# Routing kept as a table in memory that is written group by group, expert weights split behind the attention, tiles added into x2 in memory

## The reference, cut to what matters

```python
NB, LQ, LC, D = 32, 112, 375, 256       # batches, queries, context rows, width
x = x + tanh(g_xattn) * attention(ctx, layernorm(x))      # 16 heads of 64; keys: ctx and x, 487 rows
xf = layernorm(x).reshape(T, D)                           # T = 32 * 112 = 3584 tokens
gate_scores = softmax(xf @ gate_w)                        # 8 experts
topk_scores, topk_idx = top_k(gate_scores, 2)
topk_scores = topk_scores / sum(topk_scores)
h = gelu(einsum('td,edf->etf', xf, w1) + b1[:, None, :])  # F = 1024
y = einsum('etf,efd->etd', h, w2) + b2[:, None, :]
out = einsum('kt,ktd->td', topk_scores.T, y[topk_idx.T, arange(T)])
return x + tanh(g_ffn) * out
```

## Time and profile before

| | us |
|---|---|
| median of 3 runs (lowest, highest) | 1881.23 (1879.61, 1881.39) |
| the profiled execution | 1880.83 |
| its span, first to last instruction | 1879.1 |
| PE busy | 1657.4 (88%) |
| DVE busy | 1348.8 (72%) |
| ACT busy | 1186.2 (63%) |
| POOL busy | 1185.2 (63%) |

### The profile page before, as it was taken

The page is one execution under the profiler, slowest core; times in us unless marked ns, Lnnn a source line. Parts: engine busy times, 40 slices in busy tenths (PEclk is TensorE's granted clock), DMA queues, the critical chain, the costliest instruction groups (busy, mean ns, idle before and its releaser), DMA issues. The chain is left out here.

```text
span 1879.1 us, 42970 instructions
## 1 busy us (share of the span) xinstructions
PE 1657.4 (88%) x15031; PEld 1161.6 (62%) x15032; DVE 1348.8 (72%) x3173; ACT 1186.2 (63%) x2666; POOL 1185.2 (63%) x1297
## 2 busy tenths in 40 slices
PE   2899999999999999999999999997303999999980
PEld 0456666666666666666666666665202999989970
DVE  5777877778777787777877778775495666666646
ACT  2587887778877787777877778776244333333320
POOL 4477778777787777877778777767163433434420
PEclk9999999999999999999999999998556999999995
DMA  4267767667777776666766667667454111111119
GB/s 132 50 132 143 152 138 139 138 142 152 138 138 138 142 153 138 136 140 142 154 138 137 139 142 142 129 128 151 124 178 154 51 45 50 47 47 50 45 36 292
DMA packets 599543, 233.20 MB, mean 124 GB/s; under 512 B 534064, under 2 KB 584016, under 8 KB 598992
## 3 DMA queue, kind: packets, MB, share of 16 engines
q1 hardware_dynamic: 592656, 212.67, 52.7%
q0 software_dynamic: 6720, 18.36, 3.2%
HBM read 78.66 MB, written 20.19 MB: 53 GB/s over the span
## 5 line engine op out<-in xcount | busy, mean ns | idle before, releaser
L279 POOL TENSOR_TENSOR p_parts<-p_f,p_parts 112x487 f16<-112x487 f32 x512 | 559.6, 1116 | 185.6 <-ACT p_parts L373 185.6
L364 ACT ACTIVATE p_f<-scores_ps,shift 112x487 f32<-112x487 f32 x512 | 337.7, 664 | 7.9 <-DVE passed L494 4.2
L494 DVE TENSOR_SCALAR_CACHE_REDUCE passed<-scores_ps 112x487 f16<-112x487 f32 x512 | 308.0, 658 | 30.2 <-PE scores_ps L645 30.2
L401 ACT ACTIVATE k_hi<-proj_ps 128x488 fp32r<-128x488 f32 x256 | 148.0, 578 | 256.1 <-PE proj_ps L627 256.0
L1010 ACT ACTIVATE space<-h_ps,b_sb,undo 128x256 f32<-128x256 f32 x280 | 142.6, 559 | 233.4 <-PE h_ps L1239 231.0
L528 DVE SCALAR_TENSOR_TENSOR v_sb<-proj_ps,v_sb 128x512 f16<-128x512 f32 (+1 forms) x256 | 176.9, 691 | 140.6 <-ACT v_sb L415 139.4
L373 ACT ACTIVATE p_parts<-p_f 112x487 f16<-112x487 f32 x512 | 275.8, 607 | 0.0
L522 DVE TENSOR_TENSOR k_lo<-proj_ps,k_hi 128x488 fp32r<-128x488 f32 x256 | 169.0, 660 | 91.4 <-ACT k_hi L401 91.2
L676 PE MATMUL pv_ps<-v_sb,pt_sb 128*128 128x128 f16 x2048 | 218.2, 221 | 7.6 <-DMA pt_sb<-p_parts 4.8
L627 PE MATMUL proj_ps<-kv_hi,wkv_hi 128*128 128x488 f16 x512 | 191.4, 374 | 28.7 <-POOL kv_lo L306 13.5
L627 PE MATMUL proj_ps<-wkv_hi,kv_hi 128*128 128x512 f16 (+1 forms) x512 | 194.3, 379 | 0.3
(11 more groups left out here) (222 smaller groups left out, 4017.1 us busy)
## 6 DMA issues: line engine op xcount, KB each, us to landing
w_part<-in_L_ffn_w_dram SPq DMA_DIRECT2D x64, 256.0 KB, 3.5
stage<-in_L_ffn_w_dram SPq DMA_DIRECT2D x32, 512.0 KB, 4.5
ctx_sb<-in_ctx_dram SPq DMA_DIRECT2D x32, 375.0 KB
space<-y_rows SPq DMA_DIRECT2D x32, 224.0 KB, 4.7
pt_sb<-p_parts SPq DMA_TRANSPOSE x256, 4.0
x_sb<-in_x_dram SPq DMA_DIRECT2D x32, 112.0 KB
res_sb<-in_x_dram SPq DMA_DIRECT2D x32, 112.0 KB, 5.3
x_dram<-x_sb SPq DMA_DIRECT2D x32, 112.0 KB, 2.9
```

What stands on the lines that cost most here:

```text
L279: pool.tensor_tensor(p_parts[0:LQ, p % PS, h, 1, 0:LK], p_f[0:LQ, p % 2, h, 0:LK], p_parts[0:LQ, p % PS, h, 0, 0:LK], ALU.subtract).then_i ...
L364: act.activation(p_f[0:LQ, p % 2, h, 0:LK], scores_ps[n][0:LQ, 0:LK], ACT.Exp, bias=shift[0:LQ, p // 2 % 2, n:n + 1], scale=-1.0, accum_ou ...
L401: act.activation(k_hi[:, j], ps[:, 0:LKP], ACT.Copy).then_inc(kq_high, 1)
L494: dve.tensor_scalar(passed[0:LQ, n], scores_ps[n][0:LQ, 0:LK], P_SHIFT, None, ALU.add, ALU.min, accum_out=shift[0:LQ, p // 2 % 2, n:n + 1] ...
```

## The change: what it does

The two parts become one program without a barrier. (1) Attention: the steps behind PV are given by a table of stages for each batch (`USUAL`, `LATE` for batch 29, `EARLY` for 30 and 31, whose last products go to their own PSUM banks), and the drain is 20 steps. (2) Routing is done inside the attention. The batches form seven groups of 8, 8, 8, 4, 2, 1 and 1. For each group DVE makes the 0/1 vectors (`choose`), PE counts with one product more than there are batches (L1210, L1212), DVE turns counts into places in a table (`rank_entries`), and POOL writes (token, weight), 8 bytes each, into a table in memory with one indirect DMA of 112 rows per batch and choice, 64 in all, a batch per step. Each expert owns 28 rows of 128 entries; entries that nobody writes name a spare row and weight 0. Behind the attention one indirect read fetches the 70 rows in use and PE transposes them. (3) The maximum of the weights' parts is taken up to step 28 * 8, the scales are computed there, and the 32 units are loaded and split at fixed steps: 0, 1, 2 at steps 250, 252, 254, units 3 to 22 one in each step from 256 on, 23 to 25 before the tiles, the last six in the iterations of the first tiles. Always ACT makes the high half and DVE the low one. PE waits only for the experts that a tile can use. (4) Tiles: all 35 are written out. ACT weighs y by the table's weight (two more instructions to a tile), and POOL adds the rows into x2 in memory by indirect DMAs with an addition; each tile's adds wait until the last tile's have landed. (5) The last stage is four copies from memory to memory, 3.67 MB.

```diff
+USUAL = dict(zip(STAGES, (13, 21, 22, 23, 24, 25, 26, 26, 27, 28, 29, 31, 32, 33)))
+EARLY = dict(zip(STAGES, (13, 14, 15, 16, 17, 18, 19, 20, 21, 22, 23, 23, 24, 25)))
+LATE = dict(USUAL, hot=27, share=28, prefix=28, rank=29, entry=30)
+GROUPS = ((0, 8), (8, 16), (16, 24), (24, 28), (28, 30), (30, 31), (31, 32))
+SPLITS = {PAIRS - 6: 0, PAIRS - 4: 1, PAIRS - 2: 2}
+SPLITS.update({PAIRS + n: 3 + n for n in range(20)})
+BEFORE_TILES = (23, 24, 25)
+TILE_SPLITS = {-2: 26, -1: 27, 0: 28, 1: 29, 2: 30, 3: 31}
+LOADS = {t + 1: u + 4 for t, u in SPLITS.items()}
+            def load_unit(u):
...
+                if 4 <= u < 28 or u == 31:
+                    sp.wait_ge(unit_low, u - 3 if u < 28 else 29)
...
+                sp.dma_start(staged, unit_source(u)).then_inc(unit_loaded[unit_slot(u)], 16)
...
+            sp.dma_start(tanh_g[:, 1:2], g_f.partition_broadcast(128)).then_inc(small_loaded, 16)
...
+                if t == PAIRS - NP - 1:
+                    for u in range(4):
+                        load_unit(u)
+                if t in LOADS:
+                    load_unit(LOADS[t])
...
+            per = TOKENS // 4
+            for n in range(4):
+                sp.dma_start(out.rearrange("b p d -> (b p) d")[n * per:(n + 1) * per].rearrange("(q r) d -> q (r d)", q=128),
+                             sums[n * per:(n + 1) * per].rearrange("(q r) d -> q (r d)", q=128)).then_inc(out_stored, 16)
...
+                for ob in entries_at(t):
...
+                    pool.wait_ge(rank_done, n + 1)
+                    for k in range(TOPK):
+                        pool.indirect_dma_start(table.rearrange("r (n w) -> (r n) w", w=2), bass.IndirectOffsetOnAxis(ap=place_i[0:LQ, ob, k:k + 1], axis=0),
+                                                entry[0:LQ, ob, k], None).then_inc(entered, 16)
+            pool.wait_ge(row_known, 1)
+            pool.wait_ge(entered, NB * TOPK * 16)
+            pool.wait_ge(out_done, NB)
+            pool.indirect_dma_start(slots_sb[0:HALVES, :], None, table, bass.IndirectOffsetOnAxis(ap=table_row[0:HALVES, :], axis=0)).then_inc(slots_read, 16)
...
+            def add(t):
+                pool.wait_ge(y_weighed, t + 1)
+                if t >= 1:
+                    pool.wait_ge(summed[(t - 1) % 2], ((t - 1) // 2 + 1) * 32)
+                for a in range(2):
+                    n = 2 * t + a
+                    pool.indirect_dma_start(sums, bass.IndirectOffsetOnAxis(ap=sums_row[:, n:n + 1], axis=0), yw_sb[:, t % 2, a], None, compute_op=ALU.add).then_inc(summed[t % 2], 16)
...
+                if t in SPLITS:
+                    unit_high_of(SPLITS[t])
...
+                for n in groups_at("prefix", t):
...
+                    nc.tensor.matmul(ps[0:LQ, 264:264 + wide], before_me[0:LQ, 0:LQ], rows[:, 0:wide], start=True, stop=False)
+                    for d in range(1, last - first + 1):
+                        final = nc.tensor.matmul(ps[0:LQ, 264 + 8 * d:264 + wide], ones[0:LQ, 0:LQ], rows[:, 0:wide - 8 * d], start=False, stop=(d == last - first))
-            pe.wait_ge(w_split, UNIT_COUNT // 4 * 3)
-            pe.wait_ge(w_split_pool, UNIT_COUNT // 4)
+                    if n < E:
+                        pe.wait_ge(unit_low, 4 * (n + 1))
```

More of the change, by code:

```diff
@@ L31 @@
 LAG = 4
+REGION = 16384
+EXPERT_WORDS = 8192
+PARTS = 4 * E
+UNIT = 1024
 def span(t):
     return t // NP, t % NP
-STEPS = range(-3 * NP, NB * NP + 3 * NP)
+STEPS = range(-3 * NP, NB * NP + 20)
 PAIRS = NB * NP
@@ new lines, in program @@
+        base = sb("base", [128, E])
+        place = sb("place", [128, 8, E])
+        picked = sb("picked", [128, 8, TOPK, E])
+        rank = sb("rank", [128, 8, TOPK])
+        place_i = sb("place_i", [128, NB, TOPK], I32)
+        entry = sb("entry", [128, NB, TOPK, 2])
+        peaks = sb("peaks", [128, PARTS, 2])
+        b1_rows = sb("b1_rows", [E * KF, 128])
+        b1_sb = sb("b1_sb", [128, E, KF])
+        table_fill = xn_sb
+        spare_fill = x2_sb
+        count_i = sb("count_i", [128, 2, E], I32)
@@ L350, in _ @@
+            for t in range(TILES + 1):
+                if t + 2 < TILES:
+                    pool.wait_ge(xt_done, t + 1)
+                    gather(t + 2)
+                if t >= 1:
+                    add(t - 1)
         @block.scalar
         def _(act):
-            act.wait_ge(small_loaded, 16 * 6)
+            act.wait_ge(small_loaded, 16 * 7)
             act.activation(tanh_g[:, :], tanh_g[:, :], ACT.Tanh).then_inc(tanh_done, 1)
@@ new lines, in _ @@
+            s_then(dve.scalar_tensor_tensor(out=reached[HS, 1], in0=tile_end[HS, :], scalar=tile_of[HS, 0:1], in1=less[HS, :], op0=ALU.is_le, op1=ALU.mult))
+            s_then(dve.tensor_reduce(found[HS, :], reached[HS, :, 0:E - 1], AX.X, ALU.add))
+            dve.tensor_scalar(table_row[HS, :], found[HS, 1:2], row_no[HS, :], None, ALU.add).then_inc(row_known, 1)
+            for u in BEFORE_TILES:
+                unit_low_of(u)
+            dve.wait_ge(slots_turned, 1)
+            dve.tensor_copy(tile_expert[:, :], tail_bank[0:1, 256:256 + HALVES:2])
@@ L694, in _ @@
-                if ob is not None:
+                for ob in batches_at("xnt", t):
+                    ended = [n for n, (first, last) in enumerate(GROUPS) if last == ob and ob < NB - 2]
+                    if ended:
+                        pe.wait_ge(placed, ended[0] + 1)
+                    if t == CHAIN + 9:
+                        pe.wait_ge(f_moved, 5)
                     pe.wait_ge(xn_done, ob + 1)
                     for k in range(KD):
-                        last = nc.tensor.transpose(tail_ps[:, k * LQ:(k + 1) * LQ], xn_sb[0:LQ, ob % 2, k * 128:(k + 1) * 128], ident[0:LQ, 0:LQ])
+                        last = nc.tensor.transpose(tail_ps(ob)[:, k * LQ:(k + 1) * LQ], xn_sb[0:LQ, ob % 2, k * 128:(k + 1) * 128], ident[0:LQ, 0:LQ])
```

1117 lines of the change are left out of this document (524 added, 593 removed).

## The result

The kernel before ran in 1880.42 us (median of 4, 1878.1 to 1881.39), the changed one in 1850.41 us (1849.45 to 1851.1): ratio 0.9841, interval 0.983 to 0.9853. The forecast was 1831 in a range of 1793 to 1868, and faster. It is faster, inside the range, and by 30 us where 49 were forecast. The span of the profiled execution went from 1879.1 to 1849.4, 29.7 less. Where these come from is read at four places, as in the prediction.

The account below looks back on a forecast made before the run. PE's products were taken to bound attention and tiles, with time to gain in the drain, routing and last stage. First h -19.8, ramp +1, end -30.6 gave -49.4 from 1879.1; plus 1.7 outside the span, 1831 us, range 1793 to 1868.

Parts of the forecast that it names:

- Entries, +24: Attention, POOL: entry DMAs at 1.28 exceed the round by 11.6 a group, less 3.4 reserve; 8 for each of three groups.
- Rival A: Entries cost POOL little: 24 becomes 4 in the attention, 11 becomes 4 in the last steps; 1804 us, chance 0.24.
- D: Rival: routing stays on POOL's path, entry DMAs costing 2.19 as beside a DVE split; +50, 1881 us, chance 0.05.
- Prefix products, +7: Attention, PE: 32 small fp32 products at up to 0.28 each, 9.0 in all; taken as +7 us, bounds 4 and 10.
- Table operations, +2: Attention, DVE: some 15 short operations per group, mostly beside PE, may delay emptying a bank; +2 us, bounds 0 and 6.
- Start, +1: Start: SP spreads one more scalar over 128 partitions ahead of DVE's first maximum; +1 us, between 0 and 3.5.
- Last steps, +11: Attention's last steps: 7 for group four's entries on POOL, 4 for unit loads; +11 us, bounds 0 and 20.
- Last PV: End of attention: the last PV moves from 1319 to 1364 through start, products, table operations, entries and last steps.
- Last PV to first h, 52.5: Routing: units' pace sets 1408, the table's path is hidden behind it; first h at 1416.5, 19.8 us earlier.
- End, 28: Behind the last y: DVE, ACT, adds, landing and a copy of 16; 28 against 58.6, -30.6 us, bounds -35 and -20.
- rival C: Tiles: serial adds set the pace, period 2.6 plus landing, counting from a landing of 8.3; at 12, 1957 us; chance 0.06.
- Ramp +1: First tile iterations: six units left to split, where DVE has some 4 us free in 10.9; +1 us, bounds 0 and 6.

Follow-up runs that it names:

- the eight traces: Traces of kernels with the changed kernel's start left as it was; the lag at batch 2 against the kernel before was 1.4 to 3.4 us.
- The new places: Unit splits moved out of batch 31's route, and copies on SP moved, against the changed kernel: 1840.06 us, ratio 0.9783 to the kernel before.

## Why the prediction was right, and where it was off

- **Entries, +24 of bounds 0 to 36.** Measured 31.6, 7.6 more, near the upper bound. The price of 1.28 was right (by rows it would have been 1.14, not the "1.2 to 1.3" beside it), and so was the excess over a round, 11.6. The step that failed is the 3.4 taken off each group as reserve behind POOL: 0.9 for ACT and 2.5 for the second bank. The groups cost 11.9, 9.9 and 9.9, so 0 to 1.7 was given in place of 3.4; which of the two terms failed wasn't isolated. Spread out, the same issues cost 2.9. Rival A (cheap entries) needed them to fit as they stood; they fit only one per round. Of D, the 2.19 beside a DVE split did not come in the middle of the attention (median 0.95); in the last steps and the route six of 16 took 1.74 to 3.56.
- **Prefix products, +7.** 0.196 each by 32 is 6.3. **Table operations, +2**: three steps of 1.1 here, 4.5 for four if the fourth is alike; which of the group's work makes them wasn't isolated. **Start, +1**: 3.0 in the profiled execution, 2.5 over the eight traces. Not priced at all: four steps of 0.5 ahead of batches 7, 11, 15 and 19. They stand behind the four extra weight parts that PART_STEPS adds at steps 33, 65, 97 and 129; that is their place only, no run took them away.
- **Last steps, +11.** 12.3, of which group 3's entries 8.9 (predicted 7) and the rest 3.4 (predicted 4).
- **Last PV** at 1377.6, not 1364: 13.6 late, of which the entries 7.6, the start 2, the extra parts 2, and 1.3 the last steps; groups 0 to 2's products and table work came to 8.6 of the 9 taken for four groups, and some 1 stays without a name.
- **Last PV to first h, 52.5.** Measured 62.6. This is the second step that failed: "writing them and reading the table back are hidden behind units 21 to 25; if units were free, that path would set 1400". The path is batch 31's norm, transposes, choice and ranks with a split in every step, and each of ten splits (1.28), and each wait for its load, delays the path's next link. I priced units and path as two lines of which the later wins; on one engine in program order they are one line. The new places show it: 10.2 earlier. And x2 stands 17.7 behind the last PV, not 11: the transpose of o, taken as 4, had landed 8.5 after its issue (1381.8 to 1390.3), at a DMA share of 0.97 from 1381 to 1391 and with unit loads on the same queue ahead and behind; that the loads made it late is likely, not shown. The units' own pace was priced well: from x2 to the last of the 26, 30.4 where 33 were taken. From there to the first h it was 14.5, not 8.5, because the table was not in. So 6.7 for x2, -2.6 for the pace and 6.0 for the path make the 10.1. The path by itself was too short as well: with 1400 in place of 1408 the first h would stand 44.5 behind the last PV, and with the splits moved it still stood 52.9 behind. "The first h set by the table's path or by DVE's order" is one of the signs of being wrong that the prediction names.
- **End, 28.** 22.0 from DVE's step behind the true last y. The copy with its completion took 13.4 where I had 19. Here the forecast was right by luck: I set 28 against 58.6, which began a tile's y too early; against the true 53.2 the forecast would have been -25. The -30.6 agrees with -31.2 because the two errors cancel. The Trainium skill ("DMA: Bandwidth & Descriptors", "Where 436 GB/s comes from") gives about 358 GB/s for a core's memory, and I took reads and writes to share it, which made 20.5 of the copy. They moved 3.67 MB each way in 13.4, 548 GB/s together, so the trace does not bear this out. The Trainium skill says in the same page, in the note under "Measured", that the figure is a core's part when both cores of a pair stream, and here one core runs.
- **Adds.** Landing 4.0 (taken: 4), POOL 1.66 each and not 1.0; the period of about 8 lies below 10.9, so rival C never came near. (With a landing of 2.3 the end would have been 1.7 earlier, not the 1.6 of the prediction.)
- **Ramp +1**: -2.4. PE waits for no unit, and the granted clock in the first 24 us was 0.88, against 0.80 before. What raised it wasn't tested.

So the stages were right in their order and the sum was 19.7 too low: +13.6 and +10.1 at the first h, -3.4 in the ramp and -0.6 at the end, of the 49.4 forecast. The time lies in the range because the range was wide (75 us), and the agreement at the end is two errors that cancel.

## What to carry to other kernels

Work put on an engine with a quarter of its time idle costs nothing only if it comes in portions that fit the idle time of one round; a burst pays nearly the whole excess of every round, and a reserve that the engine behind is thought to give should be counted as nothing until a run shows it. Filler work between the links of a latency-bound path is on the path when both run on one engine in program order: put it where that engine waits for another. Before a stage's length is taken from the chain of waits, look in the timeline whether its last product is the last one of the kernel.

## What the runs showed of the hardware

In the middle of the attention an indirect DMA of 112 rows of 8 bytes occupied POOL for 0.95 us (0.94 to 1.21), and the next started 1.25 to 1.51 behind it; with 56 rows it was 0.93 (0.91 to 1.18), and with 128 rows of 1 KB 1.00. Of the 16 in the last steps and the route, six took 1.74 to 3.56, and each of the six began while one of DVE's 128x1024 splits was running; two others that did so took 1.02 and 1.25. An indirect DMA that adds takes 1.66 (1.55 at the very end) and lands in 4.0, against 2.42 for a plain scatter. A copy within memory moved 3.67 MB in 13.4 us with the DMA engines at 0.87, and a second queue shortened it by at most 0.3. With the splits in their new places, in one pair of traces, the table's read was 3.0 faster and the gather behind it 3.0 slower when 512 KB loads were held back from the first and let go beside the second.
